# First layer's state in 128 partitions, and the second layer's first projections placed among the first layer's last MLP part

## What is computed

```python
def mamba2(h, ...):                     # both layers, other sizes
    zxbcdt = h @ W_in
    z, xBC, dt = ...                    # dt = softplus(dt + dt_bias)
    xBC = silu(causal_depthwise_conv(xBC, conv_w, conv_b))
    x, Bmat, Cmat = ...
    def step(state, inp):               # per head: state (headdim x D_STATE)
        return state * dA_t + dt_t * outer(x_t, B_t)
    y = states . Cmat + D * x
    return rmsnorm(y * silu(z)) @ W_out

xn = _layernorm(x)
x = x + _L0_attn_ref(xn, ...) + _L0_ffn_ref(xn, ...)   # mixer and MLP, tree
xn = _layernorm(x)
x = x + _L1_attn_ref(xn, ...) + _L1_ffn_ref(xn, ...)   # mixer, experts
```

## Time and profile before

| | |
|---|---|
| median of 3 runs | 1532.46 us (1532.32 to 1533.2) |
| the profiled execution | 1534.23 us, its span 1532.4 us, mean granted PE clock 0.972 |
| PE, DVE, ACT, POOL busy | 94%, 68%, 50%, 35% of the span |
| chain that ended last | PE 63%, issue 16%, DVE 10%, POOL 8% |
| layer 1 | from 0 to 742 us, a part of some 83 to 86 us |
| layer 2's mixer begins | 742 us |

### The profile page before, as it was taken

How to read it: one execution, slowest core, us unless ns; L and a number is a source line. 1 busy time by engine, 2 the same in 40 slices (tenths; PEclk the granted TensorE clock), 3 DMA queues, 4 the chain that set the end, 5 groups by cost and what they waited for, 6 DMA issues and landing times.

```text
span 1532.4 us, 22928 instructions
## 1 busy us (share of the span) xinstructions
PE 1438.8 (94%) x7443; PEld 1063.4 (69%) x7443; DVE 1045.9 (68%) x2390; ACT 761.9 (50%) x1600; POOL 535.7 (35%) x631
## 2 busy tenths in 40 slices
PE   6899999999999999998698999999899999999996
PEld 4566767676766767677355555555578888888895
DVE  6978686867769686842687887878756465555542
ACT  4262533426262533522376676777656555555552
POOL 1344243342524234341123233332425343544343
PEclk9999999999999999998799998999999999999998
DMA  6120201203030201100411212211025333533322
GB/s 216 62 70 15 97 28 57 68 4 120 0 110 14 97 27 44 67 20 23 170 30 66 68 39 70 66 47 61 32 91 111 71 67 87 111 74 74 83 50 28
DMA packets 71847, 100.92 MB, mean 66 GB/s; under 512 B 13000, under 2 KB 58192, under 8 KB 71760
## 3 DMA queue, kind: packets, MB, share of 16 engines
q1 hardware_dynamic: 59472, 82.77, 16.6%
q0 software_dynamic: 12288, 17.05, 6.6%
HBM read 74.30 MB, written 25.49 MB: 65 GB/s over the span
## 4 chain that ended last, share of the span: by engine, by line
PE 63%; issue 16%; DVE 10%; POOL 8%; ACT 1%; DMA 1%; SPq 0%; DVEq 0%; POOLq 0%; ACTq 0%
PE bank L2160 59%; DVE u L1529 3%; POOL yb L960 2%; POOL Xs L952 2%; POOL ry L968 1%; PE bank L2269 1%; PE bank L2538 1%; DVE am L1973 1%; PE bank L2237 1%; POOL out L1018 1%; PE bank L2366 1%; POOL xg L991 1%; DVE xo L1690 1%; PE bank L2295 0%; DVE h2Tl L1697 0%
## 5 line engine op out<-in xcount | busy, mean ns | idle before, releaser
L2119 DVE TENSOR_TENSOR aml<-m0big,amh 128x512 fp32r<-128x512 f32 x128 | 88.0, 688 | 176.0 <-ACT amh L1385 175.9
L1018 POOL DMA_INDIRECT out<-EW,IDX x64 | 103.6, 1619 | 221.3 <-DVE EW L2114 206.7
L1380 ACT ACTIVATE m0big<-bank,eb 128x512 f32<-128x512 f32 x128 | 87.9, 687 | 162.8 <-PE bank L2160 147.2
L2160 PE MATMUL bank<-w2h,amh 128*128 128x256 f32 x512 | 147.9, 289 | 0.0
L2160 PE MATMUL bank<-w2h,aml 128*128 128x256 f32 x512 | 144.7, 283 | 0.0
L2160 PE MATMUL bank<-w2l,amh 128*128 128x256 f32 x512 | 144.6, 283 | 0.0
L1135 ACT ACTIVATE am<-bank,b 128x512 f32<-128x512 f32 x64 | 44.0, 687 | 151.8 <-PE bank L2160 151.2
L2160 PE MATMUL bank<-EW,am 128*128 128x256 f32 x512 | 115.8, 379 | 0.0
L2160 PEld LDWEIGHTS bank<-EW,am 128*128 128x128 f32 x512 | 97.2, 190 | 13.5 <-ACT am L1135 0.3
L2160 PEld LDWEIGHTS bank<-w2h,amh 128*128 128x128 f32 x512 | 97.6, 191 | 8.3 <-issue 5.8
L2160 PE MATMUL bank<-xTh,w1h 128*128 128x512 f32 x256 | 102.1, 399 | 0.6 <-DVE xTl L2036 0.6
(11 more groups left out here) (347 smaller groups left out, 3729.6 us busy)
## 6 DMA issues: line engine op xcount, KB each, us to landing
EW<-in_e_w SPq DMA_DIRECT2D x16, 1024.0 KB, 5.5
dA0b<-dA_d SPq DMA_DIRECT2D x16, 512.0 KB, 3.7
E<-dA_d SPq DMA_DIRECT2D x16, 512.0 KB, 5.5
m0big<-dA_d SPq DMA_DIRECT2D x16, 512.0 KB, 4.7
xin<-in_L_attn_x SPq DMA_DIRECT2D x8, 512.0 KB
xp<-in_L_attn_x SPq DMA_DIRECT2D x8, 512.0 KB, 3.8
rows_d<-xo SPq DMA_DIRECT2D x8, 512.0 KB, 3.0
x_d<-xb SPq DMA_DIRECT2D x8, 512.0 KB, 4.1
```

Source lines behind the costliest of these rows:

```text
L1018: g.indirect_dma_start(out=out_rows, out_offset=bass.IndirectOffsetOnAxis(ap=IDX[:, 4 * u + c:4 * u + c + 1], axis=0), in_=ye[:, q, c, :], ...
L1380: a.activation(am2[:, j % 2, :], bank[j % 2][:, :], ACT.Gelu, bias=eb1[:, u // 2, j:j + 1]).then_inc(gelu_sig.sem, 1)
L2119: v.tensor_tensor(aml[:, j % 4, :], am2[:, j % 2, :], amh[:, j % 4, :], ALU.subtract).then_inc(am_low.sem, 1)
L2160: return t.matmul(out_, lhsT, rhs, start=first, stop=last)
```

## The change

Five edits.

1. Layer 1's state lies in 128 partitions x 256: heads 0 to 3 in partitions 0 to 63, heads 4 to 7 in 64 to 127, as in layer 2. `recur` makes inter as two products of 256 columns and the state as two of 64 partitions x 256, with the wait for `half` between; C is needed a second time in partitions 64 to 127 (`second_c` on ACT, once a step), and the decays in the same split (`exs`, two copies on DVE in `start`, once a step).
2. DVE's `h2T_low` comes after three convolutions instead of four.
3. hT and x1 of layer 2's step 0 are loaded by SP in part 7, ahead of its last two stores, instead of after the barrier.
4. The in-projections of layer 2's step 0 (`in_proj1`, `raw1`), its convolutions (`conv1`) and their silu (`silu1`) are issued in the end of part 7 and in the last part, with banks 0 and 1 instead of 2 and 3.
5. z and the transposes of chunk 0 (`z_xt1(0, 0)` on PE, `chunk1(0, 0)` on ACT) are issued at the end of the last part, ahead of the nT transposes and copies.

```diff
@@ signals, buffers
-DF0, DT0, DN, DB0 = 13, 15, 9, 11
+DF0, DT0, DN, DB0 = 15, 15, 9, 11
...
-        Ct = sb("Ct", [64, T])
+        CC = sb("Ct", [P, T])
+        Ct, C2 = CC[0:64, :], CC[64:P, :]
+        exs = sb("exs", [P, CH * 4])
...
@@ SP
             later_decays_of(STEPS - 1)
+            s0.zs.wait_ge(sp, STEPS - 1, CH)
+            nT_stored.wait_ge(sp, 0, 16)
+            load_hT(0)
+            xn_sig.wait_ge(sp, STEPS - 1, CH)
+            x1_stored.wait_ge(sp, 0, 16)
+            load_x1(0)
             store_back(STEPS - 2)
...
@@ ACT
+            def second_c(L, s, i):
+                n, cp = L.state, L.cpart
+                s.t1.wait_ge(act, i, 0)
+                a.activation(C2[0:n, :], s.u_buf[cp:cp + n, 4, :], ACT.Silu).then_inc(s.c2.sem, 1)
...
@@ ACT step0
+                if f is None:
+                    raw1(0, 2)
+                    raw1(0, 3)
                 if b is not None:
                     h2T_copies()
+                if f is None:
+                    raw1(0, 4)
...
+                    second_c(L, s, f)
                     chunk(L, s, f, 0)
...
+                    if f is None:
+                        silu1(0, c)
+                        if c + 1 == CH:
+                            silu1(0, 4)
...
                     raw(L, s, n, 0)
+                elif f is not None:
+                    raw1(0, 0)
+                else:
+                    chunk1(0, 0)
...
@@ DVE start
+                for half in range(2):
+                    rows = slice(64 * half, 64 * (half + 1))
+                    ch.put(v.tensor_copy(exs[rows, :].rearrange("p (c h) -> p c h", c=CH),
+                                         s.ex_buf[rows, 2, 0:n].rearrange("p (c h) -> p c h", c=CH)
+                                         [:, :, 4 * half:4 * half + 4]))
+                ch.see(dve)
                 s.S.wait_ge(dve, i, 0)
-                v.tensor_scalar(S[:, :], S[:, :], flags[0:64, bass.ds(i, 1)], None,
-                                ALU.mult).then_inc(s.S.sem, 1)
+                v.tensor_scalar(S1, S1, flags[:, bass.ds(i, 1)], None, ALU.mult).then_inc(s.S.sem, 1)
...
@@ DVE sums
-                ch.put(v.tensor_tensor(s3, s3, ex3[0:n, 2, :].unsqueeze(2).to_broadcast([n, nh, hp]), ALU.mult))
+                s3 = S1.rearrange("p (h e) -> p h e", h=nh // 2)
+                ch.put(v.tensor_tensor(s3, s3, exs[:, 4 * c:4 * c + 4].unsqueeze(2).to_broadcast([P, nh // 2, hp]),
+                                       ALU.mult))
...
-                v.tensor_tensor(S[:, :], S[:, :], p[0:n, :], ALU.add).then_inc(s.S.sem, 1)
+                v.tensor_tensor(S1, S1, p[:, 0:2 * P], ALU.add).then_inc(s.S.sem, 1)
...
@@ DVE step0
-                    for j in range(4):
+                    for j in range(3):
                         conv(L, s, f, j, dve0)
                         keep_halo(L, s, f, j)
                 if b is not None:
                     h2T_low()
+                if f is None:
+                    for j in range(5):
+                        conv1(0, j)
                 if f is not None:
-                    conv(L, s, f, 4, dve0)
-                    keep_halo(L, s, f, 4)
+                    for j in range(3, 5):
+                        conv(L, s, f, j, dve0)
+                        keep_halo(L, s, f, j)
...
             rest_of_mixer()
+            dve1.begin(0)
+            sets[0].halo.wait_ge(dve, STEPS - 1, 5)
+            v.memset(xbuf[:, :, 0:3], 0.0).then_inc(s1.halos.sem, 1)
+            s1.halos.wait_ge(dve, 0, 1)
             step0(None, None, STEPS - 1)
...
@@ PE recur
-                filled(mm(p[:, :], s.Ct_buf[:, cols(c)], S[:, :]), s, L, f"inter{c}")
-                p = open_front(pe, L, s, i, f"state{c}")
+                mm(p[:, 0:2 * P], s.Ct_buf[:, cols(c)], S1[0:64, :]).then_inc(s.half.sem, 1)
+                r = open_front(pe, L, s, i, f"state{c}")
                 s.bs.wait_ge(pe, i, c + 1)
                 s.xs.wait_ge(pe, i, c + 1)
-                filled(mm(p[0:64, :], Bs[:, q, :], Xs[:, q, :]), s, L, f"state{c}")
+                mm(r[0:64, 0:2 * P], Bs[:, q, :], Xs[:, q, 0:2 * P])
+                filled(mm(r[64:P, 0:2 * P], Bs[:, q, :], Xs[:, q, 2 * P:4 * P]), s, L, f"state{c}")
+                s.half.wait_ge(pe, i, c + 1)
+                s.c2.wait_ge(pe, i, 1)
+                filled(mm(p[:, 2 * P:4 * P], C2[:, cols(c)], S1[64:P, :]), s, L, f"inter{c}")
```

More of the change, by code:

```diff
@@ L746, in load_w2 @@
                 sp.dma_start(ws2, d["e_w2"][e].rearrange("(k p) n -> p k n", p=P)).then_inc(w2_loaded.sem, 16)
[L748 to L750 removed]
+            load_hT(1)
+            load_x1(1)
             s1.dAT.wait_ge(sp, 0, 2)
@@ new lines, in chunk1 @@
+            def chunk1(i, c):
+                q, n = c % 2, CH * i + c
+                p = front1(act, "z", n)
+                if n == 0:
+                    for last in (s0.yg, s0.xs, s0.xdt, s0.xd, s0.y0):
+                        last.wait_ge(act, STEPS - 1, CH)
+                s1.yg.wait_ge(act, i, c - 1)
+                a.activation(zs[:, q, :], p[:, :], ACT.Silu).then_inc(s1.zs.sem, 1)
+                p = front1(act, "xt", n)
+                s1.xs.wait_ge(act, i, c - 1)
+                s1.y0.wait_ge(act, i, c - 1)
+                a.activation(Xsb[:, q, :], p[:, :], ACT.Copy).then_inc(s1.xsb.sem, 1)
+                for k in range(NH1):
+                    ins = a.activation(XD[:, q, P * k:P * (k + 1)], p[:, P * k:P * (k + 1)], ACT.Copy,
+                                       scale=W[1]["D"][:, k:k + 1])
+                ins.then_inc(s1.xd.sem, 1)
@@ L1680, in mixed0, with op, conv1 @@
                                        op1=ALU.add).then_inc(s.x2.sem, 1)
+            def op(ins):
+                dve1.put(ins)
+                dve1.see(dve)
+            def conv1(i, j):
+                blk, ub, w = (j - 1) % 5, UB[i % 2], W[1]["conv"]
+                s1.xb.wait_ge(dve, i, 2 * (j + 1))
+                for k in range(3):
+                    ins = v.scalar_tensor_tensor(out=ub[:, blk, :], in0=xbuf[:, blk, k:k + T],
+                                                 scalar=w[:, blk, k:k + 1], in1=ub[:, blk, :], op0=ALU.mult,
+                                                 op1=ALU.add)
+                    if k < 2:
+                        op(ins)
+                    else:
+                        ins.then_inc(s1.u.sem, 1)
+                s1.u.wait_ge(dve, i, j + 1)
+                if i % (STEPS // NB) == STEPS // NB - 1:
+                    v.memset(xbuf[:, blk, 0:3], 0.0).then_inc(s1.halo.sem, 1)
+                else:
+                    v.tensor_copy(xbuf[:, blk, 0:3], xbuf[:, blk, T:T + 3]).then_inc(s1.halo.sem, 1)
             def step0(n, f, b):
@@ L1815, in _ @@
             dve.wait_ge(phase, 5)
-            dve1.begin(0)
-            def op(ins):
-                dve1.put(ins)
-                dve1.see(dve)
             v.memset(SS[:, :], 0.0).then_inc(prepped, 1)
-            v.memset(xbuf[:, :, 0:4], 0.0).then_inc(prepped, 1)
             v.memset(thrf[:, :], 0.0).then_inc(prepped, 1)
@@ L2055, in _ @@
                                  EX[rows, 2, :].rearrange("p (t h) -> p t h", h=NH1)[:, :, 2 * half:2 * half + 2]))
-            for j in range(1, 5):
-                conv1(0, j)
             count(0)
@@ L2359, in step0 @@
                     in_proj(L, s, n, 0)
+                elif f is not None:
+                    in_proj1(0, 0)
+                else:
+                    z_xt1(0, 0)
                 if b is not None:
@@ L2370, in step0 @@
                     in_proj(L, s, n, 1)
+                elif f is not None:
+                    in_proj1(0, 1)
                 if b is not None:
@@ L2501, in _ @@
             t.transpose(INTRA[:, 0:P], DA, ident[:, :]).then_inc(s1.dAT_full.sem, 1)
-            for j in range(2, 5):
-                in_proj1(0, j)
             chunk1(0, 0)
```

211 lines of the change are left out of this document (97 added, 114 removed).

## The result

| | before | changed |
|---|---|---|
| median beside each other | 1532.83 us (4 runs) | 1507.54 us (4 runs, 1504.56 to 1509.84) |
| ratio | | 0.9831, 95% interval 0.9809 to 0.9853 |
| profiled execution, its span | 1534.23, 1532.4 us | 1508.89, 1507.0 us |
| mean granted PE clock | 0.972 | 0.976 |

The change is 25.3 us faster, by the medians and by the profiled executions alike; 1505.9 had been forecast. Measured once more, the same kernel gave 1504.78 (ratio 0.982, 0.9798 to 0.9843).

The account below looks back on a forecast made before the run. PE was taken to bound most of the kernel, with few waits in layer 1 and pauses between the layers. Terms of -7.5, -2.6, -1.6, -3.9 and -11 sum to -26.6 us, from 1532.46 to 1505.9; range 1498 to 1517.

Parts of the forecast that it names:

- Term A: Parts 1 to 7, before the first up: h2T_low after three convolutions ends most of PE's wait for DVE, -7.5 us.
- Rival 2: At the ups, ACT takes DVE's place as what PE waits for, so the -7.5 us gain goes: 1513.4; chance 0.12.
- Term B: Recurrence on PE: a chunk falls from 2.05 to 1.96 us, 28 chunks in PE-bound parts, -2.6 us.
- Rival 5: State in 128 partitions saves nothing, as an operation costs by something other than its columns: 1510.1; chance 0.02.
- Term C: Part 0, where DVE is the bound: cheaper operations on S, less two small copies, -1.6 us.
- Term D: End of part 7 to the barrier: layer 2's projections and z fill PE's pauses, PE at full clock, -3.9 us.
- rival 1: PE's clock falls between the parts all the same, +8 instead of -3.9 us: 1517.8; chance 0.17.
- Term E: Start of layer 2: without in-projections there, the count begins 11.5 us and the first scan 10.2 us earlier; -11 us taken.
- Rival 3: Layer 2's start gain is lost because DVE or POOL sets the pace or decay rows land late: 1516.9; chance 0.08.
- Rival 4: In layer 1's recurrence PE halts for Xs, one 2.3 us pause a part plus slow passes: 1539.5; chance 0.03.

Follow-up runs that it names:

- e1: Kernel before with only the low part of the transposed rows moved to after three convolutions; 7.4 us faster by the ratio, executions 1523.18 to 1531.47 us.
- e2: Kernel before with only layer 1's state in 128 partitions; 12.6 us faster by the ratio, executions 1521.09 to 1531.82 us.
- e4: Changed kernel with three unused 512-column products on PE after chunk 0's recurrence in part 0; median 1503.99 us, runs 1501.1 to 1505.8.
- e8: Kernel before with three unused 512-column products on PE after chunk 0's recurrence in part 0; gained nothing, part 1 reached at 172.92 us.
- e5: Kernel before with the 128-partition state and the reordered convolutions, nothing of the boundary between the layers; median 1518.56 us.
- e9: The changed kernel measured once more, word for word, beside the kernel before; 1504.78 us, ratio 0.982.
- e3: Kernel before with only the early loads, early first projections and early z, old state and convolution order; 12.9 us faster by the ratio.
- e6: e5 plus five unused products of in-projection size where the change issues layer 2's projections, layer 2 still doing all its work; median 1513.67 us.
- e7: Changed kernel with z and the transposes of chunk 0 put back into layer 2; 1505.88 us.

## Why the prediction held, and where its terms did not

From the profile before to the changed one, in the order of time: parts 0 and 1 to the first `xo<-xb` +2.0 (-1.6 up to PE's z at 33 us, +3.6 behind it), from there to part 7's last `xb` -12.7, D -3.1, E -11.0, from the count to the end -0.6: -25.4, the difference of the spans. The forecast was -26.6, but two terms were off in opposite directions.

- **Term A** (-7.5 forecast): near, and too small. The wait in the earlier trace rows went, as e1 shows alone: 1.39 a middle part, 7.1 over the six steps from part 1 to part 7, where 1.07 a part, 6.4, was forecast. ACT's am, for which I gave 0.3 a part back, did not appear (another 0.5 of the sum, "the odd tenth in the chain before", has no row behind it): its wait is 1.4 per four parts in both kernels. Rival 2 fell with it.
- **Term B** (-2.6): the mechanism was right, the size wrong. The step "0.09 a chunk" took 1.96 from one chunk of layer 2, which held 0.13 of a wait; the chunk takes 1.83, 0.22 less, and e2 has a pitch 0.96 shorter alone, 5.7 us over the six steps. What shrinks is Xs,Bs: four passes into the two halves of a bank take 371.21 - 370.63 = 0.58, two passes of 512 columns took 1.00 in the chunk of the earlier trace rows; the two halves of S,Ct cost 0.62 + 0.63 against 1.05 and give 0.2 of it back. Rival 5 fell.
- **Term C** (-1.6): the saving is there, 1.7 by e4 against e8, and more than that by e5 against e1 (part 1 at 165.39 and 168.83, of which part 1's own share of the state is about 1). That the size fits is in part luck: the gain of 0.25 an operation from the earlier trace rows holds only where POOL is idle; beside it the scaling saved 0.5. The step that failed was leaving PE's clock out of part 0: the profiled execution paid for the fall behind the pause of 2.68. It is not a price of the change as such, since e9 has 165.24 with it: from PE's z at 33 us on, e9 is 2.3 shorter than the profile before. With e9's profile in place of the first the difference of the spans is 30.8.
- **Term D** (-3.9): -3.1 and -2.7 in the two profiles, -2.3 in e3, and 1.3 less than each of these against e8's 53.52, whose code is the same as before there. So the term was too large. In its steps, profile after against profile before: -0.7 up to the first up where -1.0 was forecast (xo came 9.9 behind the last `xb` of part 7 in both kernels, not 0.5 earlier), -1.6 from there to the last `xb` (-2.3; here lies the 0.48 for ACT's read, which was to come in time), -0.8 at the end (-0.6). The clock stayed up; rival 1 fell. The rule of the Trainium skill that it was weighed against ("TensorE: Matmul & The Clock Gate", PE-mode transpose) was not tested: no run has only transposes in a pause. On the table load the trace sided with the row, not with the price of 2.66 from "ScalarE: Activation LUTs", What ACT_TABLE_LOAD costs, of the Trainium skill: 688.35 + 1.28 = 689.63, and the read begins at 689.64; in front of the load ACT's last operation ends at 688.33.
- **Term E** (-11): -11.0 to the count and -10.3 to the first scan, where 11.5 and 10.2 were worked out. The count then took 0.7 longer, since its first operation lay beside POOL's Xs. But edit 5's share in it is nothing, which the step had not looked at apart; how the rest divides between the early loads and the early projections was not run. Rival 3 fell. Rival 4, the halt in the recurrence, did not show: PE waits for Xs nowhere in the loop.

The sum came out within 2 us partly by luck: over the six steps A and B gave 12.7 where 8.7 was forecast, and parts 0 and 1 were 2.0 later where some 3 earlier was forecast (C, and one part's A and B), and D gave 0.8 less.

## What to carry to other kernels

A pause of PE of 2 to 3 us cost here its own length and then the slow passes behind it, and that second price varied by execution: 5.9 us more in one execution than in another for the same pause. Try to fill such pauses with work that has to be done anyway, or even with work that nobody uses, but with less than the pause holds, and look whether the next pause only inherits the fall. Cost a recurrence from several chunks at full clock, not from one. Before a stretch's gain is given a number, look at the same stretch in two executions of the same code: D differed by 1.25 us between two.

## What the runs showed that I had not expected

- The same pause, 2.68 us, was followed by about 3.4 us of low clock in five profiles (e9's z took 3.37, three of its four passes slow) and by about 17 us in two, one kernel being among both. In the long one PE was busy 12.00 of the 12 us from 52 to 64 and still at 0.50 for most of it. The later parts repeat to 0.01 us (pitch 84.02 or 84.03 in all of them), so the scatter of the executions does not come from there.
- Five unneeded products of an in-projection's size (1.72 each) made a stretch 3.5 us shorter (e6 against e5).
- Operations that touch next to nothing were slow beside POOL. DVE's cand, 128x3, took 0.15 in the earlier trace rows and 0.89 at 741.05, while POOL made this:

```profile
740.84 1.08 POOL L962 TENSOR_TENSOR Xs<-Xsb,lp 128x512 f32<-128x512 f32 x1 [9.32 <-DVE lp L2091]
```

  The same operation took 0.16 in e7, where that Xs ran later.
